# An opening rebuilt on one core of a Trainium2 chip: smaller pieces of the loads, the splits shared out anew, the products in order of arrival

## What is computed

```python
out = conv1d(x, weight, groups=4, padding=4)              # 9 taps, 32 channels
out = out + (cond @ c_weight.T)[:, :, None] + bias[None, :, None]
base = out @ base_W.T + base_b                            # over L = 512
logits = out @ router_W.T + router_b                      # 15 routes
topk_p, topk_i = top_k(softmax(logits), 8)
w = einsum('btk,btke->bte', topk_p, onehot(expert_map[topk_i]))
h = einsum('btd,erd->bter', out, A)                       # 8 experts, rank 16
lora = einsum('bter,eor->bto', h * w[..., None], B) * 2.0
return x + base + lora
```

## Time and profile before

| | |
|---|---|
| median of 3 runs | 201.48 us (200.59 to 201.67) |
| the profiled execution's own time | 201.99 us |
| its span, from the first to the last instruction | 200.2 us |
| mean granted TensorE clock | 0.991 |
| busy in the span: PE, PEld, DVE, ACT, POOL | 95%, 91%, 82%, 38%, 72% |
| bytes moved | 27.78 MB, 139 GB/s on the mean |

### The profile page before, as it was taken

One profiled execution on the slowest core, in us unless ns is written; L12 is line 12 of the kernel. 1 busy time (PEld: TensorE's weight loads), 2 busy tenths in 40 slices (PEclk: granted clock), 3 DMA queues, 4 the chain that ended last, 5 costly groups with the idle time before them and its releaser, 6 DMA issues.

```text
span 200.2 us, 4334 instructions
## 1 busy us (share of the span) xinstructions
PE 190.6 (95%) x1304; PEld 182.0 (91%) x1304; DVE 163.1 (82%) x548; ACT 76.5 (38%) x196; POOL 143.1 (72%) x113
## 2 busy tenths in 40 slices
PE   7798699999999999999999999999999999998993
PEld 2667499999999999999999999999999999997992
DVE  1399898888888889898888888888998889775662
ACT  5164253344444343334444443433344444122210
POOL 5359988777777778887777777788777777852520
PEclk9999879999999999999999999999999999999999
DMA  6994044334445444434443444444334223333312
GB/s 163 296 393 146 21 138 143 128 114 147 119 149 165 158 158 155 145 121 129 138 139 122 158 158 158 158 140 147 124 122 154 67 90 108 105 105 110 105 52 105
DMA packets 18955, 27.78 MB, mean 139 GB/s; under 512 B 2112, under 2 KB 10176, under 8 KB 18944
## 3 DMA queue, kind: packets, MB, share of 16 engines
q1 hardware_dynamic: 18688, 27.11, 41.2%
q0 software_dynamic: 112, 0.28, 0.8%
q10 hardware_dynamic: 144, 0.26, 0.4%
HBM read 19.25 MB, written 8.39 MB: 138 GB/s over the span
## 4 chain that ended last, share of the span: by engine, by line
PE 85%; POOL 4%; DMA 4%; DVE 3%; issue 1%; ACT 1%; SPq 1%; DVEq 0%; ACTq 0%
PE wide_ps L486 54%; PE conv_banks L469 15%; PE wide_ps L510 11%; DMA x_in<-x_start 4%; POOL is_expert L420 2%; PE conv_banks L486 2%; PE hwt_bank L497 2%; POOL terms_lo L404 1%; POOL y_lo L410 1%; DVE y_rows L588 1%; PE odd_bank L440 0%; POOL map_f L417 0%; DVE y L672 0%; PE conv_banks L510 0%; DVE xr L583 0%
## 5 line engine op out<-in xcount | busy, mean ns | idle before, releaser
L486 PE MATMUL wide_ps<-wide_hi,y_hi 128*128 128x400 f32 (+1 forms) x248 | 80.6, 329 | 1.0 <-DVE xr L583 0.9
L486 PE MATMUL wide_ps<-wide_lo,y_hi 128*128 128x400 f32 (+1 forms) x248 | 76.5, 313 | 0.5 <-DVE wide_lo L221 0.5
L486 PE MATMUL wide_ps<-wide_hi,y_lo 128*128 128x400 f32 (+1 forms) x248 | 76.5, 313 | 0.0
L404 POOL TENSOR_TENSOR terms_lo<-terms,terms_hi 128x768 fp32r<-128x768 f32 x28 | 51.7, 1847 | 30.8 <-ACT terms_hi L334 30.8
L486 PEld LDWEIGHTS wide_ps<-wide_hi,y_hi 128*128 128x128 f32 x248 | 46.6, 189 | 3.6 <-issue 1.2
L486 PEld LDWEIGHTS wide_ps<-wide_lo,y_hi 128*128 128x128 f32 x248 | 46.8, 190 | 0.8 <-DVE wide_lo L221 0.8
L486 PEld LDWEIGHTS wide_ps<-wide_hi,y_lo 128*128 128x128 f32 x248 | 46.5, 189 | 0.0
L399 POOL TENSOR_TENSOR xr<-xr,biases_sb 128x512 f32<-128x512 f32 x32 | 41.7, 1302 | 6.5 <-DMA xr<-x_rows 6.4
L410 POOL TENSOR_TENSOR y_lo<-y,y_hi 128x512 fp32r<-128x512 f32 x32 | 41.5, 1296 | 3.1 <-ACT y_hi L341 3.0
L348 ACT ACTIVATE hw_hi<-hwt_bank 128x128 fp32r<-128x128 f32 x32 | 8.9, 277 | 88.1 <-PE hwt_bank L497 88.1
L341 ACT ACTIVATE y_hi<-y 128x512 fp32r<-128x512 f32 x32 | 20.2, 632 | 17.8 <-PE wide_ps L486 17.0
(11 more groups left out here) (91 smaller groups left out, 266.5 us busy)
## 6 DMA issues: line engine op xcount, KB each, us to landing
xr<-x_rows SPq DMA_DIRECT2D x32, 256.0 KB, 2.7
out<-xr SPq DMA_DIRECT2D x31, 256.0 KB, 2.0
even<-x_even SPq DMA_DIRECT2D x28, 132.0 KB, 2.5
terms<-x_odd SPq DMA_DIRECT2D x28, 128.0 KB, 2.8
wide_sb<-wide_w SPq DMA_DIRECT2D x2, 656.0 KB, 9.0
x_in<-x_start SPq DMA_DIRECT2D x2, 260.0 KB, 5.4
x_in<-x_start SPq DMA_DIRECT2D x1, 520.0 KB, 10.6
biases_sb<-biases POOLq DMA_DIRECT2D x1, 263.5 KB, 6.8
```

The costliest lines, as they stand in the source:

```text
L404: nc.gpsimd.tensor_tensor(terms_lo[i % 2][:, :, :, :], terms[i][:, :, :, :], terms_hi[i % 2][:, :, :, :].bitcast(F32), ALU.subtract)\
L486: mm = nc.tensor.matmul(sums_of(t, k)[:, b, 0:columns[1] - columns[0]], a[k % 2][:, r, :], w[:, r, columns[0]:columns[1]], start=r == 0 an ...
```

## The change

The opening is written anew; the steps of later tiles stay as they are.

- **Loads.** `cond` carries the condition's weights once (32 columns) instead of repeated (256), is issued by ACT behind `conv_w`, and POOL repeats it in SBUF (`cond_w_sb`). The first eight batches of `x` are two arrays with contiguous rows, `wide` comes in four pieces instead of two, and `biases` is issued by SP behind the second eight batches instead of by POOL.
- **Splits.** All of `x_hi` is made on ACT. POOL splits runs 0 and 1 of `wide`, DVE runs 2 and 3. On ACT `y_high(0)` stands behind three runs of `wide_high` instead of two.
- **TensorE.** The first convolutions are ordered by operand: high by high, rest of the weights, the condition, rest of `x`. `linear(0)` runs the rest of `wide` for runs 0 and 1 ahead of the rest of `y`. The convolution of step 0 stands behind the front bank of `linear(1)`.
- **POOL.** `y_low(1)` follows `y_low(0)` directly; of the table only `map_f` is made there, and eight memsets of one column each make `expert_ids`. The split of `conv_sum` is moved behind it. The copy of the condition's weights is added.
- **DVE.** `is_expert` is one compare of 128 x 120; it and `up_lo` stand between the two `add_condition` of the second eight batches. `cond_sb` is made in one instruction. `add_condition` has the same sums, but writes `y_rows` in contiguous runs of 32 and reads PSUM with a stride of two, where before it read contiguously and wrote with a stride of 32.

The diff, cut to its core (declarations of tiles and semaphores, the first convolutions, the condition's bias and the arrays on the host are left out; a line of "..." marks what is left out):

```diff
@@ -244,14 +249,12 @@
-            sync.dma_start(x_in[0][:, :, 0:Q, :], x_start[0, :, :, 0:Q, :])\
-                .then_inc(x_first_in, 16)
-            sync.dma_start(cond_in_sb[:, :], cond).then_inc(cond_in, 16)
-            sync.dma_start(x_in[0][:, :, Q:, :], x_start[0, :, :, Q:, :]).then_inc(x_second_in, 16)
-            for r in range(0, RUNS, 2):
-                sync.dma_start(wide_sb[:, r:r + 2, :], wide_w[:, r:r + 2, :])\
-                    .then_inc(wide_in[r // 2], 16)
-            sync.dma_start(x_in[1][:, :, :, :], x_start[1]).then_inc(x_third_in, 16)
+            for i in range(2):
+                sync.dma_start(x_in[i][:, :, :, :], x_first[i]).then_inc(x_loaded[i], 16)
+            for r in range(RUNS):
+                sync.dma_start(wide_sb[:, r, :], wide_w[:, r, :]).then_inc(wide_in[r], 16)
+            sync.dma_start(x_in[2][:, :, :, :], x_pair).then_inc(x_loaded[2], 16)
+            sync.dma_start(biases_sb[:, :], biases.partition_broadcast(P)).then_inc(biases_in, 16)
@@ -294,22 +297,21 @@
+            act.dma_start(cond_in_sb[:, :], cond).then_inc(cond_in, 16)
...
-            act.wait_ge(conv_summed, 1)
-            nc.scalar.activation(conv_hi[:, :, BLOCKS, :], conv_sum[:, :, :], ACT.Copy)\
-                .then_inc(conv_sum_hi_ready, 1)
-            act.wait_ge(x_second_in, 16)
-            nc.scalar.activation(x_hi[0][:, :, Q:, :], x_in[0][:, :, Q:, :], ACT.Copy)\
-                .then_inc(x_hi_ready, 1)
+            def x_high(i):
+                act.wait_ge(x_loaded[i], 16)
+                nc.scalar.activation(x_hi[i][:, :, :, :], x_in[i][:, :, :, :], ACT.Copy)\
+                    .then_inc(x_hi_ready, 1)
...
-                    act.wait_ge(wide_in[r // 2], 16)
+                    act.wait_ge(wide_in[r], 16)
@@ -348,14 +350,17 @@
-            wide_high(range(RUNS // 2))
+            x_high(0)
+            x_high(1)
+            wide_high(range(RUNS - 1))
             y_high(0, 0)
-            wide_high(range(RUNS // 2, RUNS))
-            act.wait_ge(x_third_in, 16)
-            nc.scalar.activation(x_hi[1][:, :, :, :], x_in[1][:, :, :, :], ACT.Copy)\
-                .then_inc(x_hi_ready, 1)
+            wide_high(range(RUNS - 1, RUNS))
+            x_high(2)
...
+            act.wait_ge(conv_summed, 1)
+            nc.scalar.activation(conv_hi[:, :, BLOCKS, :], conv_sum[:, :, :], ACT.Copy)\
+                .then_inc(conv_sum_hi_ready, 1)
@@ -385,15 +390,16 @@
+            for e in range(E):
+                nc.gpsimd.memset(expert_ids[:, e:e + 1], float(e)).then_inc(ids_ready, 1)
+            pool.wait_ge(cond_in, 16)
+            nc.gpsimd.tensor_copy(
+                cond_w_sb[:, :, :, :],
+                cond_w_in_sb.unsqueeze(2).to_broadcast([P, HALVES, BP, CH])).then_inc(cond_w_ready, 1)
             pool.wait_ge(conv_w_in, 16)
+            pool.wait_ge(x_lo_first, 1)
...
-            pool.wait_ge(conv_sum_hi_ready, 1)
-            nc.gpsimd.tensor_tensor(conv_lo[:, :, BLOCKS, :], conv_sum[:, :, :],
-                                    conv_hi[:, :, BLOCKS, :].bitcast(F32), ALU.subtract)\
-                .then_inc(conv_sum_lo_ready, 1)
-            pool.dma_start(biases_sb[:, :], biases.partition_broadcast(P)).then_inc(biases_in, 16)
@@ -411,15 +417,15 @@
-            split_wide(pool, nc.gpsimd, range(1))
+            split_wide(pool, nc.gpsimd, range(RUNS // 2), wide_lo_first)
             y_low(0, 0)
+            y_low(1, 1)
...
-            pool.wait_ge(map_ready, 1)
-            for e in range(E):
-                nc.gpsimd.tensor_scalar(is_expert[:, e, :], map_f[:, :], float(e), None,
-                                        ALU.is_equal).then_inc(map_ready, 1)
-            y_low(1, 1)
+            pool.wait_ge(conv_sum_hi_ready, 1)
+            nc.gpsimd.tensor_tensor(conv_lo[:, :, BLOCKS, :], conv_sum[:, :, :],
+                                    conv_hi[:, :, BLOCKS, :].bitcast(F32), ALU.subtract)\
+                .then_inc(conv_sum_lo_ready, 1)
@@ -538,11 +552,15 @@
+                for r in runs[:RUNS // 2]:
+                    pe.wait_ge(wide_lo_first, r + 1)
+                    linear(0, 0, (r,), products=(W_REST,))
...
-                pe.wait_ge(wide_lo_ready, RUNS)
+                pe.wait_ge(wide_lo_second, RUNS // 2)
                 for bank, done in ((FRONT_BANK, front_done), (NEXT_BANK, linear_done)):
-                    linear(0, 0, runs, (bank,), (W_REST,), (RUNS - 1, W_REST)).then_inc(done, 1)
+                    linear(0, 0, runs[RUNS // 2:], (bank,), (W_REST,), (RUNS - 1, W_REST))\
+                        .then_inc(done, 1)
@@ -561,11 +579,13 @@
+                    if isinstance(t, int) and t == 1:
+                        conv(0, 0, 0)
...
-                if up_to_tile(t, TILES - 5):
+                if from_tile(t, 1) and up_to_tile(t, TILES - 5):
@@ -586,9 +606,9 @@
-                    rows.rearrange("p n (a k) -> p n k a", a=2),
-                    sums.rearrange("p n (k a) -> p n k a", a=2),
-                    c.unsqueeze(2).unsqueeze(3).to_broadcast([P, batches, MK, 2]), ALU.add)\
+                    rows.rearrange("p n (a k) -> p n a k", a=2),
+                    sums.rearrange("p n (k a) -> p n a k", a=2),
+                    c.unsqueeze(2).unsqueeze(3).to_broadcast([P, batches, 2, MK]), ALU.add)\
@@ -709,19 +725,28 @@
-            split_wide(dve, nc.vector, range(1, RUNS))
-            dve.wait_ge(up_hi_ready, 1)
-            nc.vector.scalar_tensor_tensor(out=up_lo[:, :], in0=up_sb[:, :], scalar=LORA_SCALE,
-                                           in1=up_hi[:, :].bitcast(F32), op0=ALU.mult,
-                                           op1=ALU.subtract).then_inc(up_lo_ready, 1)
-            dve.wait_ge(x_hi_ready, 2)
+            split_wide(dve, nc.vector, range(RUNS // 2, RUNS), wide_lo_second)
+            dve.wait_ge(x_hi_ready, 3)
             for h in range(HALVES):
-                x_low_first(1, (every, h, every, every))
+                x_low_first(2, (every, h, every, every))
...
+                if h == 0:
+                    dve.wait_ge(up_hi_ready, 1)
+                    nc.vector.scalar_tensor_tensor(out=up_lo[:, :], in0=up_sb[:, :],
+                                                   scalar=LORA_SCALE,
+                                                   in1=up_hi[:, :].bitcast(F32), op0=ALU.mult,
+                                                   op1=ALU.subtract).then_inc(up_lo_ready, 1)
+                    dve.wait_ge(map_ready, 1)
+                    dve.wait_ge(ids_ready, E)
+                    nc.vector.tensor_tensor(
+                        is_expert[:, :, :],
+                        map_f[:, :].unsqueeze(1).to_broadcast([P, E, ROUTES]),
+                        expert_ids[:, :].unsqueeze(2).to_broadcast([P, E, ROUTES]),
+                        ALU.is_equal).then_inc(is_expert_ready, 1)
```

More of the change, by code:

```diff
@@ L47, with build @@
 WARM_UP, WARM_BETWEEN, WARM_END = 9, 7, 4
-def build(nc, x_start, x_even, x_odd, x_rows, conv_w, cond, wide_w, up_w, biases, expert_map, out):
+def build(nc, x_first, x_pair, x_even, x_odd, x_rows, conv_w, cond, wide_w, up_w, biases, expert_map, out):
     ctx = ExitStack()
@@ L131, in build @@
         cond_in = sem("cond_in")
-        wide_in = [sem(f"wide_in{i}") for i in range(RUNS // 2)]
+        cond_w_ready = sem("cond_w_ready")
+        wide_in = [sem(f"wide_in{i}") for i in range(RUNS)]
         up_in = sem("up_in")
@@ L216, in unit_of, with split_wide @@
             return (k + ahead) % 2, p + pairs, (k // 2 + pairs) % 2
-        def split_wide(eng, ops, runs):
+        def split_wide(eng, ops, runs, ready):
             for r in runs:
@@ L793 @@
     given = {
-        "x_start": blocks[:START],
+        "x_first": first,
+        "x_pair": blocks[1],
         "x_even": units[..., 0::2],
```

86 lines of the change are left out of this document (47 added, 39 removed).

## The result

| | before | after |
|---|---|---|
| median | 201.65 us of 20 runs (200.59 to 202.65) | 202.55 us of 20 runs (201.65 to 203.87 without one of 234.0) |
| ratio, 95% interval | | 1.0034 (1.0018 to 1.0050) |
| profiled execution | 201.99 us | 202.13 us |
| first product of `linear(2)` | 31.95 | 31.57 |
| from there to the end of the span | 168.2 | 168.7 |

What follows compares the result with a forecast made beforehand. DVE's chain from the second y_rows to linear(2) was taken as the bound: 1.5 us from an earlier second y_rows plus 0.35 from its shorter duration gave 1.85 us, so about 199.6 us against 201.48; range 197.8 to 201.6.

Steps and rivals of the forecast that it cites:

- What bounds the kernel: Opening, up to linear(2) at 31.95 us: DVE's list from the second y_rows (21.78) to tile 0's sum (31.80) decides.
- Loads: Start of the kernel: the four pieces of wide land at 9.5, 10.3, 11.1 and 11.9 us.
- early bound of 7.5: Loads at the start: piece 0 of wide lands not before 7.5 us, two us less than the 9.5 forecast.
- rival B: wide lands at the early bound, second batches start by 15.7; 1.2 us more gain, 198.4 us; chance 0.13.
- `y_lo(0)` at 14.7, second batches 16.9 to 20.0: POOL ends y_lo(0) at 14.7 us; TensorE's second eight batches start 1.75 us earlier, at 16.9, and end at 20.0.
- rival D: POOL's y_lo(0) ends after 16.4 us and starves TensorE, which runs at half clock; 202.6 us; chance 0.14.
- `y_rows` at 0.70: DVE's y_rows of 128 x 512 in the new pattern takes 0.70 us instead of 1.06 to 1.14.
- DVE between the halves: Between the second batches' two y_rows: up_lo 0.69 and is_expert 0.28 us, so the second y_rows starts at 20.3.
- 168.2 us, which I take as unchanged: From the first product of linear(2) to the end of the span: 168.2 us, the same after the change.
- rival C: TensorE falls to half clock in holes before the second batches, costing about 1.7 us; 201.3, no change; chance 0.21.
- Sum: Whole kernel: 1.85 us gained, profiled execution 201.99 to 200.1, or about 199.6 against a median of 201.48.

Runs made afterwards that it cites:

- experiment 7: experiment 1 with the load of expert_map issued by SP behind biases instead of by POOL at 2.2 us; 199.25 us, ratio 0.9837, in two groups.
- experiment 1: The changed kernel with one more wait: POOL holds back terms_lo until DVE has made is_expert; 199.60 us, ratio 0.9874.
- experiment 5: The kernel before with only the new add_condition pattern (y_rows written in contiguous runs of 32, PSUM read with stride two); 201.37 us, ratio 0.9972.
- experiment 3: The kernel before with is_expert as one compare on DVE ahead of the first y_rows, instead of eight on POOL; 203.40 us, ratio 1.0069.
- experiment 4: experiment 3 with POOL's y_lo(1) made to wait for x_lo of the second eight batches; 202.68 us, ratio 1.0052.
- experiment 6: The changed kernel with POOL's first split of terms and first adding of base_b replaced by plain copies; 200.38 us in one run.
- experiment 11: experiment 7 with eleven warming products of zeros instead of nine; 198.48 us, ratio 0.9844.
- experiment 2: The changed kernel with up_lo on POOL behind terms_lo and is_expert on DVE ahead of the second batches' first y_rows; 199.75 us, ratio 0.9887.
- experiment 8: experiment 2 with the load of expert_map issued by SP behind biases; 199.21 us, ratio 0.9864, in two groups.
- experiment 9: experiment 2 with ten warming products of zeros instead of nine; 199.68 us, ratio 0.9878.
- experiment 10: experiment 8 with POOL making map_f ahead of y_lo(1), which waits for x_lo of the second eight batches; 198.37 us, ratio 0.9853.
- experiment 12: experiment 10 with eleven warming products of zeros instead of nine; 198.33 us, ratio 0.9833.

## Why the prediction was wrong

- **What bounds the kernel**: right. DVE's list from the second `y_rows` to the sum of tile 0 sets `linear(2)`, before and after (idle 0.23 us, ended by DVE).
- **Loads**: right for the later pieces, wrong in shape. `wide_hi` had its first piece at 6.42 us, ahead even of the early bound of 7.5, its second only at 9.59 and its last at 11.61 (behind `y_hi`); 9.5, 10.3 and 11.9 were forecast for the landings. The doubt about rival B, that the map's load stays, was right, and experiment 7 shows what it holds back.
- **`y_lo(0)` at 14.7, second batches 16.9 to 20.0**: 11.95 + 1.89 = 13.84, and 16.31 to 19.4. Better than forecast; POOL did not starve TensorE (rival D).
- **`y_rows` at 0.70**: 0.69 and 0.68. What the prediction took from the Trainium skill on PSUM's lines, that a read with a stride of two would take the gain away, does not hold for this instruction.
- **DVE between the halves: the step that failed.** "`up_lo` 0.69 and `is_expert` 0.28": 0.97 us priced, 22.07 - 18.64 = 3.43 measured. The first price came from a row beside which POOL ran only its compares of 15 columns, the second from an instruction with an operand in PSUM. The text even put `terms_lo` at 18.0 to 19.8 and these two ahead of 20.3, side by side, and asked only whether POOL would be late for its own users. The second `y_rows` came at 22.07, not 20.3: 1.77 us, of the 1.85 forecast as gain. With 0.96 in its place (experiment 1) `linear(2)` stands at 29.29, ahead of the 30.1 forecast, and the time is 0.9874 of before. The same step failed at DVE's two splits of `wide`, priced at 1.7 us and measured at 3.32 beside `y_lo`; that it cost little is luck: the loads let them start at 11.22, so that they ended at 14.54, where 15.2 was forecast.
- **"168.2 us, which I take as unchanged"**: 168.7. The 0.38 us gained at `linear(2)` are given back over the steps that the change leaves alone, and 0.1 more; it is why the profiled execution is level with the one before and not 0.4 us faster. It comes in small parts: the same 20 steps of the loop, from one transposition of `hw` to the 20th behind it, take 161.47 - 50.78 = 110.69 us before and 161.57 - 50.49 = 111.08 after. The profile names no wait for it. By kernel: 168.2 (before, experiment 5), 168.5 to 168.7 (after, experiments 1, 3, 4, 6, 7, 11), 169.3 (2, 8, 9, 10, 12, all with `up_lo` on POOL, and 1.1 us ahead of five weight loads). What in the lists does this stays open.
- **The clock (rival C)**: a half clock came, at 26 to 29 us, not between 12 and 20, and behind a DVE chain that covers it. In the runs it still shows: 8 of the 19 had a mean clock of 0.983 or less and took 202.87 us on the mean, the 11 others (0.990 to 0.992) 202.27. The kernel before, in the 23 executions beside experiments 1 to 3 and 5, never went below 0.988; 8 of them had 0.998 or more and took 201.46, the 15 others 202.19. Executions near 0.99 are thus level (202.27 and 202.19), as the two profiled ones are; the medians differ since only the kernel before has executions at 0.998 and more, and only the changed one has them at 0.983 and less. So what rival C had in mind is a part of the slowdown. Why the clock behaves so in the executions that were not profiled is open.
- **Sum**: for the profiled execution 201.99 - 1.85 = 200.14 was forecast. The second `y_rows` came 1.77 us late (0.66 won ahead of `up_lo`, 2.46 lost in the two instructions), 0.3 were won from there to `linear(2)`, 0.5 lost behind it: 202.1. It took 202.13.

The rivals were all of waits and clock. None of them was that an instruction takes longer because of what another engine runs beside it.

## What to carry to other kernels

A duration from a row holds only beside the work that row had beside it: before moving a DVE instruction with both operands in SBUF, list what POOL runs at the new place and keep POOL back there (a wait costs one line) or choose an operand in PSUM. Taking work from POOL can be a loss, when it lets POOL's next instruction meet DVE. A broadcast of a few short rows is worth a trial behind the loads that the start needs, issued by SP; together the two steps took the slump away here.
